# Steps put apart in attention, the last group's sums by TensorE alone, bfloat16 masks, and exponentials one PSUM bank at a time

## The reference

```python
mod = silu(c) @ wmod                 # six rows of 1024 per batch: sa, ca, ga, sb, cb, gb
h = layernorm(x) * (1 + ca) + sa
q, k, v = h @ Wq, h @ Wk, h @ Wv     # rotary embedding on q and k
p = softmax(causal(q @ k.T / sqrt(32)))
x = x + ga * ((p @ v) @ Wo)
h = layernorm(x) * (1 + cb) + sb
x = x + gb * (h @ W.T + bias + sum_n coef_n * (h @ A_n.T) @ B_n.T)   # 8 LoRA pairs of rank 16
```

## Time and profile before

| | |
|---|---|
| runs | 2541.00, 2547.65, 2546.32 us, median 2546.32 |
| profiled execution | 2545.68 us, its span 2543.9 us |
| mean granted TensorE clock | 0.983 of full speed |
| busy, TensorE matmul | 2444.4 us (96%) |
| busy, VectorE | 1718.8 us (68%) |
| busy, ScalarE | 1016.9 us (40%) |
| busy, GpSimd | 1649.6 us (65%) |
| mask products of 128 columns, L249 | 733 in attention and 35 in the projection stage |
| ScalarE exponentials, L946 | 512 into p_ring, 128 into p_sum |

### The profile page before, as it was taken

How to read it: one execution, slowest core, us unless ns; L and a number is a source line. 1 busy time by engine, 2 the same in 40 slices (tenths; PEclk the granted TensorE clock), 3 DMA queues, 4 the chain that set the end, 5 groups by cost and what they waited for, 6 DMA issues and landing times. The chain is left out here.

```text
span 2543.9 us, 36463 instructions
## 1 busy us (share of the span) xinstructions
PE 2444.4 (96%) x13772; PEld 1765.2 (69%) x13772; DVE 1718.8 (68%) x2893; ACT 1016.9 (40%) x1297; POOL 1649.6 (65%) x865
## 2 busy tenths in 40 slices
PE   5999999999999999999999999897999999999998
PEld 2788888887565666566565665553688888888886
DVE  3666666777788887878878886785655455555553
ACT  3433333331565665656656665555311111111111
POOL 3543333441798998999989998794655654555543
PEclk8999999999999999999999999998899999999999
DMA  7422333351534225334233334310533333323430
GB/s 283 134 92 108 116 116 116 120 154 70 159 97 143 63 68 163 81 98 114 66 94 81 77 93 120 97 46 19 186 91 93 114 99 92 114 95 95 116 91 25
DMA packets 179706, 267.17 MB, mean 105 GB/s; under 512 B 20508, under 2 KB 113884, under 8 KB 178400
## 3 DMA queue, kind: packets, MB, share of 16 engines
q1 hardware_dynamic: 179552, 265.13, 35.4%
HBM read 183.22 MB, written 80.81 MB: 104 GB/s over the span
## 5 line engine op out<-in xcount | busy, mean ns | idle before, releaser
L1062 POOL TENSOR_TENSOR p_sum<-p_sum,p_ring 128x1024 f32<-128x1024 f32 (+2 forms) x465 | 992.2, 2165 | 109.4 <-PE ctx_ps L1116 90.4
L259 DVE TENSOR_REDUCE neg_max<-scores_q 128x1 f32<-128x512 f32 (+1 forms) x1168 | 711.6, 654 | 158.6 <-PE scores_q L246 105.0
L946 ACT ACTIVATE p_ring<-scores 128x1024 f32<-128x1024 f32 (+2 forms) x512 | 466.3, 917 | 291.6 <-DVE scores L998 222.9
L1095 PE MATMUL scores<-q_stack,k_stack 98*128 98x512 f32 (+1 forms) x1216 | 419.4, 422 | 41.4 <-ACT p_ring L946 31.3
L246 PE MATMUL scores_q<-k_stack,q_stack 96*128 96x512 f32 (+1 forms) x1473 | 441.6, 370 | 1.0 <-DVE prefetched L1025 1.0
L1095 PEld LDWEIGHTS scores<-q_stack,k_stack 98*128 98x128 f32 x1216 | 192.6, 191 | 209.1 <-ACT p_ring L946 112.0
L614 POOL TENSOR_TENSOR roped_hilo<-roped_hilo 128x512 fp32r<-128x512 f32 x80 | 105.6, 1320 | 346.9 <-ACT roped_hilo L456 346.9
L246 PEld LDWEIGHTS scores_q<-k_stack,q_stack 96*128 96x128 f32 x1473 | 268.1, 190 | 70.7 <-DVE neg_max L259 29.9
L663 PE MATMUL proj_ps<-h_hi,w_hi 128*128 128x512 f32 x768 | 306.8, 399 | 1.6 <-POOL h_lo L607 1.6
L663 PE MATMUL proj_ps<-h_hi,w_lo 128*128 128x512 f32 x768 | 300.5, 391 | 0.0
L663 PE MATMUL proj_ps<-h_lo,w_hi 128*128 128x512 f32 x768 | 300.4, 391 | 0.0
(11 more groups left out here) (168 smaller groups left out, 3763.6 us busy)
## 6 DMA issues: line engine op xcount, KB each, us to landing
q_stack<-qk_t SPq DMA_DIRECT2D x96, 512.0 KB, 6.9
qk_t<-roped_hilo SPq DMA_DIRECT2D x80, 512.0 KB, 2.8
x_in<-in_L_attn_resid SPq DMA_DIRECT2D x32, 512.0 KB, 6.6
ctx_t<-ctx_raw SPq DMA_DIRECT2D x64, 256.0 KB, 5.3
prefetched<-in_L_wmod SPq DMA_DIRECT2D x4, 4096.0 KB, 13.6
prefetched<-ctx_t SPq DMA_DIRECT2D x31, 512.0 KB, 4.1
prefetched<-inv_t SPq DMA_DIRECT2D x124, 128.0 KB, 5.5
k_stack<-qk_t SPq DMA_DIRECT2D x96, 128.0 KB, 8.8
```

The lines of the kernel that those rows point to most:

```text
L259: nc.vector.tensor_reduce(sh.negm[:, lo // HALF, hs[0]:hs[-1] + 1, i:i + 1], src, AX.X, ALU.max, negate=True).then_inc(sh.s_mx.sem, 1)
L946: nc.scalar.activation(probs(n, u), scores_of(n, u), ACT.Exp, scale=SM_SCALE).then_inc(s_ex.sem, 1)
L1062: nc.gpsimd.tensor_tensor(a, a, probs(n, u), ALU.add).then_inc(s_ap.sem, 1)
L1095: last = nc.tensor.matmul(o[a], ks[n % QS][0:KS, j * P:(j + 1) * P], qs[n % QS][0:KS, h0:h0 + per, lo:lo + w], start=True, stop=True)
```

## The change

1. Steps. The split of the first context and the LoRA factors get steps of their own: `scale` (GpSimd) stays at (26, 12), `split_hi` (ScalarE) is at (27, 10), `split_lo` (GpSimd) at (28, 3), `lora` (SP, loads) at (28, 13), `coef` (ScalarE) at (29, 10).
2. Last group. No engine adds its exponentials. `last_sums`, called behind each key tile's `values`, multiplies each of them by the ones and lets PSUM add them up; the exponentials in the ring are given free by these sums.
3. Masks. `maskS` and `identr` become bfloat16, and a first-pass unit of two heads by 256 columns gets one mask product of 2 x 128 columns behind both heads in place of one of 128 behind each.
4. Exponentials. A unit of 256 columns or more is taken by two ScalarE instructions, one for each bank, and TensorE waits for each bank by itself before it writes the scores of two units later. All others wait for the whole unit as before.

```diff
-FETCH_AT, FIRST_AT, SPLIT_AT, LORA_AT = (25, 2), (26, 3), (26, 12), (27, 3)
+FETCH_AT, FIRST_AT, LORA_AT = (25, 2), (26, 3), (28, 13)
+SCALE_AT, SPLIT_HI_AT, SPLIT_LO_AT, COEF_AT = (26, 12), (27, 10), (28, 3), (29, 10)
...
-        self.maskS = sb("mask_q_k", [P, G, P], F32R)
-        self.identr = sb("ident_r", [P, P], F32R)[:, :]
+        self.maskS = sb("mask_q_k", [P, 2, G, P], BF16)[:, 0, :, :]
+        self.identr = sb("ident_b", [P, 2, P], BF16)[:, 0, :]
...
     for a, h in enumerate(hs):
         last = nc.tensor.matmul(dst[:, a, :], qs[0:MHI, h, i * P:(i + 1) * P], ks[0:MHI, lo:lo + w],
-                                start=not first, stop=not diag or first and a == len(hs) - 1)
-        if diag and not first:
-            last = nc.tensor.matmul(dst[:, a, w - P:w], sh.identr, sh.maskS[:, 0, :], start=False, stop=True)
+                                start=not first and (a == 0 or not diag), stop=not diag or first and a == len(hs) - 1)
+    if diag and not first:
+        last = nc.tensor.matmul(dst[:, :, w - P:w], sh.identr, sh.maskS[:, 0:len(hs), :], start=False, stop=True)
...
-        s_p2, s_ex, s_pv, s_dm = count("exp_scores"), count("probs_ready"), count("values_done"), count("diagonal_masked")
-        s_av, s_ap = count("probs_added_dve"), count("probs_added_pool")
+        s_p2, s_ex, s_pv, s_dm = count("exp_scores"), count("probs_ready", 2), count("values_done"), count("diagonal_masked")
+        s_ap = count("probs_added_pool")
...
-                        if before[1] in TAIL[0] + TAIL[1]:
+                        if before[1] in TAIL[0] + TAIL[1] or before[0] == NG - 1:
                             act.wait_ge(s_sm.sem, s_sm.at(2 * before[0] + EXP_UNITS[before[1]][0] + 1))
-                        elif before[0] == NG - 1:
-                            act.wait_ge(s_av.sem, s_av.at(POOL_ADDS.index(before[1]) + 1))
...
-                nc.scalar.activation(probs(n, u), scores_of(n, u), ACT.Exp, scale=SM_SCALE).then_inc(s_ex.sem, 1)
+                p, src = probs(n, u), scores_of(n, u)
+                if w == P:
+                    nc.scalar.activation(p, src, ACT.Exp, scale=SM_SCALE).then_inc(s_ex.sem, 2)
+                else:
+                    per = len(hs) // 2
+                    for a in range(2):
+                        nc.scalar.activation(p[:, a * per:(a + 1) * per, :], src[:, a * per:(a + 1) * per, :], ACT.Exp,
+                                             scale=SM_SCALE).then_inc(s_ex.sem, 1)
...
-                elif kind == "values" and n == NG - 1:
-                    for u in QUADS[step[2]]:
-                        if u in POOL_ADDS:
-                            add(n, u)
...
-                if at >= SS:
-                    pe.wait_ge(s_ex.sem, s_ex.at(at - SS + 1))
...
                 for a in range(len(hs) // per):
                     h0 = hs[0] + a * per
+                    if at >= SS:
+                        pe.wait_ge(s_ex.sem, s_ex.at(at - SS) + a + 1)
...
+                if n == NG - 1:
+                    last_sums(q)
+
+            def last_sums(q):
+                hf, j, hs, lo, w = EXP_UNITS[QUADS[q][0]]
+                n, step = NG - 1, ("sum", NG - 1, hf)
+                if j == 0:
+                    wait_bank(pe, step)
+                for u in QUADS[q]:
+                    p = probs(n, u)
+                    for a, h in enumerate(EXP_UNITS[u][2]):
+                        last = nc.tensor.matmul(mp[BANK[step]][DH * h:DH * (h + 1), lo - hf * HALF:HALF], ones[:, :], p[:, a, :],
+                                                start=(j == 0), stop=(j == 4 * hf + 3))
+                if q == LAST_QUAD[hf]:
+                    last.then_inc(s_sm.sem, 1)
```

More of the change, by code:

```diff
@@ L119, in group_steps @@
             steps.append((("inv_in", "inv", "inv_out")[INV_AT.index(u)], n // KV - 1))
[L120 removed]
+        for kind, at in (("fetch", FETCH_AT), ("first", FIRST_AT), ("scale", SCALE_AT), ("split_hi", SPLIT_HI_AT),
+                         ("split_lo", SPLIT_LO_AT), ("lora", LORA_AT), ("coef", COEF_AT)):
             if (n, u) == at:
@@ L1161, in _ @@
                     values(n, step[2])
-                elif kind == "sum":
+                elif kind == "sum" and n < NG - 1:
                     sums(n, step[2])
```

29 lines of the change are left out of this document (9 added, 20 removed).

## The result

The changed kernel takes 2528.5 us (median of 4 runs, 2528.1 to 2530.1) against 2545.7 (4 runs, 2541.0 to 2547.7): ratio 0.9937, 95% interval 0.9924 to 0.9949. It is 17 us faster where 39 were forecast; 2528 lies in the range of 2494 to 2534. The profiled execution took 2528.8, its span 2527.0, 16.9 under the span before.

What follows compares the result with a forecast made beforehand. TensorE was taken to bound attention, GpSimd close behind. Steps 11.7, projection masks 0.6, steady groups 21.6 and last group 5 sum to 38.9 us: 2545.7 - 38.9 = 2506.8, forecast 2507 us (2497 to 2515; all terms' ends 2494 to 2534).

Steps and rivals of the forecast that it cites:

- Together 15.1 us, which go if each step finds its input ready: Groups 26 and 27: stalls at the context split and LoRA loads, 6.94 and 8.17 us, vanish once steps are put apart.
- Together 3.4: Moved GpSimd multiplies, 2.5 us each, make TensorE wait for sums: 2.3 and 1.1 us lost, bounds 0 to 5.0.
- One fewer of them is 0.10, four times a group: 0.4: First-pass units of two heads by 256 columns: merging masks saves one matmul each, 0.4 us a group.
- bfloat16 changes no column count ... I take 0: The other 18 mask matmuls: bfloat16 gains nothing, as the mask's own load already lies under the product before; 0 us.
- Rival (b): Masks themselves get cheaper and GpSimd becomes the bound: steady groups gain 28.2 in place of 21.6, 2500 us; chance 0.12.
- Rival (c): Type change between product and mask holds TensorE's array: 0.18 us a mask, 704 masks, 127 us lost, 2634 us; chance 0.07.
- The wait shrinks by 0.3: Steady group, before unit 5's product: exponentials by bank cut TensorE's 0.57 us idle time by 0.3.
- rival (a): Steady group doesn't shorten by 0.7, held by VectorE's masks, maxima rows or second waits: 2516 or 2528 us; chance 0.22.
- 0.72 a group, 21.6 in all: Steady attention groups: merged masks 0.4 plus exponentials by bank 0.3 shorten each; 21.6 us over 30 groups (0 to 28.2).
- 3.5 + 3.7 - 1.5 = 5.7: Last group, sums by TensorE: 3.5 us gained at unit 18, 3.7 at the end, 1.5 paid; less 0.8, 5 (2 to 8).
- The linear half keeps its length: Sign to look for: the stage after attention takes as long as before.
- Attention ends at about 1740: Sign to look for: in the changed kernel's trace, attention ends at about 1740 us.

## Why the prediction was wrong, point by point

- **"Together 15.1 us, which go if each step finds its input ready"**: right. 15.9 over two groups by the rows of maxima, and all of it went but 1.7. **"Together 3.4"** for GpSimd's push was too much: in group 27 TensorE waited 1.31 in place of 2.3, and in the group after the low part not at all. I had charged GpSimd for a group of 33.7, and the group stayed at 34.14; but that explains little of it, for with the steps alone, at 34.43 a group, the wait is 1.29. (The slack of 0.94 is also misread: 1645.97 less 1642.65 + 2.34 is 0.98.) Where GpSimd finds the rest stays open. Net 14.2 for 11.7, and 15.9 us by the medians of the kernel with the steps alone.
- **"One fewer of them is 0.10, four times a group: 0.4"**: right in kind, 0.28 alone. The price per mask held in three places of four; in the fourth the next wait took it. "Whatever the width" was wrong for the merged mask: with fp32r masks the next first-pass product starts 0.12 behind one of 256 columns and 0.06 behind one of 128.
- **"bfloat16 changes no column count ... I take 0"**: the step that has the wrong sign. 0.20 a group with single masks, 0.09 with merged. I looked at the load as something hidden that could not get worse. It is shorter and is started later. Rival (b), the masks get cheaper, fell with it, and its premise of a fast load was true: the Trainium skill ("TensorE: Matmul & The Clock Gate", section "Weight-path perf modes") gives about twice the speed for such loads, and 97 against 189 ns agree; what it does not follow is that time is won. Rival (c) had the right sign, with a price of 0.18 a mask where 0.004 (merged) to 0.008 (single) was measured.
- **"The wait shrinks by 0.3"**: measured 0.33, but I put the whole of it into the sum. 0.19 came back at VectorE's bank one product later. My sentence "all other products of that timeline come later than the exponential they need" asked only for exponentials; rival (a) named VectorE, and the profile had said that VectorE has no gap from unit 0 to 5. This is the step that failed: the term 0.72 a group, 21.6 in all, measured 0.29 and 8.7. Of the 0.43 missing, 0.18 are the bank, 0.14 the merge and 0.09 the type; 0.02 stays open. Rival (a) also gave 2528 us for a group that gains nothing, and 2528.5 was measured: that is luck, since the group did gain and other terms missed too.
- **"3.5 + 3.7 - 1.5 = 5.7"** less 0.8 in the last group: measured 3.1, and that size is an accident of the clock. The end was right: from unit 18's product to the end of the last copy 10.2 before and 6.6 after, 3.5 for 3.7. In the middle VectorE no longer holds up unit 18's product, but TensorE does itself, for unit 16's product has moved behind `last_sums`: from 30.9 after the last row of maxima to 34.1, and unit 18's from 35.3 to 35.7. Of this 1.6 is the lower clock in front of unit 16. In the three kernels where the clock stayed up, these products come at 32.5 and 34.2 and the last group is 4.7 shorter, close to the 5 of the forecast. What the forecast left out is the clock, which decides between 0.3 and 4.7.
- **"The linear half keeps its length"**: wrong, 6.2 longer (a term of nothing in the sum; 8.0 of stall less 1.1 and small items). I had looked at what the change computes there, and not at where it moves the code. The trace before could not show it: there the loop stands in a good place.
- **"Attention ends at about 1740"**: 1755.8. Of the 16 us late 13 are the steady groups, 2 the last group (its clock), 1.6 the start and 1.9 small items (0.6 that I had put on the projection's masks among them), less 2.5 that the steps gave more.

## What to carry to other kernels

Behind each wait that an edit shortens, read who comes next on that engine with a second engine's name: the gain is what both leave, and VectorE without a gap was such a sign here. A cheaper weight load is no gain if it is no longer started under the product before, as with the bfloat16 masks here, so a change of type between products is tested alone. A long loop (here 1699 TensorE instructions) has a place: edits far ahead of it can cost or give microseconds at each jump back. This is seen in rows "<- issue" on an engine that waited for nothing, with more packets on the instruction queue. And before a term of a few microseconds is called missed, compare the granted clock in its stretch: here it made 4.4 us of difference in one and the same last group.

## What the runs showed of the hardware

- A 128 by 128 bfloat16 weight load took 97 ns and an fp32r one 189; between 4-byte products the first began 0.01 us before its matmul and the second 0.17, and mask and next product took 0.36 us against 0.34 in one place (0.02 less to 0.02 more over all); a group became 0.20 us longer with single masks, 0.09 with merged ones.
- A loop of 1699 TensorE instructions ran without stalls where it touched seven blocks of 256, and lost 2.8 to 16.8 us at two jumps back where it touched eight, with 17 to 20 more instruction packets. At these jumps it went on 1.3 to 1.7 us after such a packet had landed, 23 times of 23.
- Two halves of a 1024-column exponential took 1.09 us (1.11 in the changed kernel) for 1.02 in one piece, as forecast from copies.
- After an equal idle time of 2.52 us the granted clock stayed at 2.4 GHz in one kernel and was at 1.2 GHz for some 6 of the next 8 us in another.
